# Two attention layers on one core: the parts of queries and keys go from one on-chip buffer straight into the score operands, without a copy in device memory

## Time and profile before

| | us |
|---|---|
| median of 3 runs (3643.35 to 3670.59) | 3657.52 |
| the profiled execution, its own time | 3658.99 |
| its span, first to last instruction | 3657.2 |
| PE busy, share of the span | 3449.0 (94%) |
| DVE busy | 2872.1 (79%) |
| ACT busy | 2484.4 (68%) |
| POOL busy | 2119.5 (58%) |
| bytes moved by DMA | 376.45 MB, mean 103 GB/s |

### The profile page before, as it was taken

The page is one execution under the profiler, slowest core; times in us unless marked ns, Lnnn a source line. Parts: engine busy times, 40 slices in busy tenths (PEclk is TensorE's granted clock), DMA queues, the critical chain, the costliest instruction groups (busy, mean ns, idle before and its releaser), DMA issues. The chain is left out here.

```text
span 3657.2 us, 79325 instructions
## 1 busy us (share of the span) xinstructions
PE 3449.0 (94%) x26824; PEld 1944.8 (53%) x26824; DVE 2872.1 (79%) x8451; ACT 2484.4 (68%) x5347; POOL 2119.5 (58%) x2340
## 2 busy tenths in 40 slices
PE   5999999999999999999689999999999999999997
PEld 2444444444444444444446666666666666666664
DVE  5899999999998999998267777677777777777773
ACT  2788888788788888887346666566666666666663
POOL 2377777677767777775745455455454554554542
PEclk7999999999999999999879999999999999999997
DMA  4344434433343444343466767767668668677761
GB/s 122 68 83 86 95 68 90 93 87 76 84 99 71 89 88 92 71 87 91 87 130 106 139 120 122 134 118 124 129 120 132 116 120 142 118 121 139 122 108 30
DMA packets 251934, 376.45 MB, mean 103 GB/s; under 512 B 21930, under 2 KB 122448, under 8 KB 251264
## 3 DMA queue, kind: packets, MB, share of 16 engines
q1 hardware_dynamic: 249484, 369.28, 53.2%
q10 hardware_dynamic: 2048, 2.10, 0.4%
HBM read 223.97 MB, written 136.95 MB: 99 GB/s over the span
## 5 line engine op out<-in xcount | busy, mean ns | idle before, releaser
L681 DVE TENSOR_REDUCE maxima<-ps_max 128x1 f32<-128x512 f32 x2048 | 1274.1, 680 | 98.2 <-PE ps_max L444 94.0
L1524 DVE CUSTOM_DVE_ANT_0 ps_max<-ps_max,mask 128x512 f32<-128x512 f32 (+3 forms) x2048 | 962.4, 515 | 353.4 <-PE ps_max L1246 350.7
L575 ACT ACTIVATE probs<-ps_rest 128x512 f32<-128x512 f32 x2048 | 1073.5, 602 | 226.7 <-PE ps_rest L457 224.1
L1397 ACT ACTIVATE probs<-ps_rest 128x512 f32<-128x512 f32 (+3 forms) x2048 | 773.4, 436 | 452.4 <-PE ps_rest L1267 400.0
L444 PE MATMUL ps_max<-k_op,q_op 48*128 48x512 f32 x2048 | 724.5, 446 | 61.8 <-DVE maxima L681 54.0
L457 PE MATMUL ps_rest<-q_op,k_op 50*128 50x512 f32 x2048 | 717.1, 441 | 0.3 <-ACT probs L575 0.2
L444 PEld LDWEIGHTS ps_max<-k_op,q_op 48*128 48x128 f32 x2048 | 340.2, 187 | 531.7 <-DVE maxima L681 411.5
L1246 PE MATMUL ps_max<-k_op,q_op 51*128 51x512 f32 (+3 forms) x2048 | 564.6, 366 | 23.8 <-DVE maxima L1524 4.0
L1267 PE MATMUL ps_rest<-q_op,k_op 53*128 53x512 f32 (+3 forms) x2048 | 559.6, 366 | 19.9 <-DMA q_op<-mrows 19.7
L478 PE MATMUL ps_pv<-probs,v_op 128*32 128x512 f32 x4096 | 543.0, 605 | 1.0 <-ACT oT L587 1.0
L1246 PEld LDWEIGHTS ps_max<-k_op,q_op 51*128 51x128 f32 x2048 | 315.4, 188 | 166.9 <-DVE maxima L1524 89.6
(11 more groups left out here) (145 smaller groups left out, 5465.3 us busy)
## 6 DMA issues: line engine op xcount, KB each, us to landing
qk_parts<-qparts SPq DMA_DIRECT2D x192, 512.0 KB, 3.2
q_op<-qk_parts SPq DMA_DIRECT2D x384, 256.0 KB, 7.8
k_op<-qk_parts SPq DMA_DIRECT2D x192, 256.0 KB, 10.5
xin<-in_x SPq DMA_DIRECT2D x32, 512.0 KB, 4.6
xres<-in_x SPq DMA_DIRECT2D x32, 512.0 KB, 4.8
x_mid<-xo SPq DMA_DIRECT2D x32, 512.0 KB, 3.2
xin<-x_mid SPq DMA_DIRECT2D x32, 512.0 KB, 7.1
xres<-x_mid SPq DMA_DIRECT2D x32, 512.0 KB, 15.8
```

Source lines behind the costliest of these rows:

```text
L575: act.activation(probs[:, quad % 2, at:at + S], ps_rest[:, bank("exp", b, p), :], ACT.Exp).then_inc(ps_out["exp"], 1)
L681: dve.tensor_reduce(at, ps_max[:, bank("max", c, k), :], AX.X, ALU.max).then_inc(ps_out["max"], 1)
L1397: act.activation(probs[quad % 2][:, at:at + nq], ps_rest[:, bank("exp", b, p), 0:nq], ACT.Exp).then_inc(ps_out["exp"], 1)
L1524: dve.tensor_tensor_reduce(row, row, mask[:, S - keys:S], 1.0, LOWEST, ALU.add, ALU.max, at).then_inc(ps_out["max"], 1)
```

## The change

The weights of the query and key projections are reordered on the host so that within each 128 output columns the dimension of a head is the slow index and the head the fast one (`by_dim`). Row p of a projection is then dimension p // 8 of head p % 8, and the 128 rows of a part, read in order, are already `[16, 8, 512]`. The loads read `qparts` on chip instead of `qk_dram`; `store_parts`, its steps in the two plans, `qk_dram` and `qk_stored` are gone. The loads wait for the splits themselves. `split_qk` now waits for the loads that read the buffer: in layer 0 those of the sequence before, in layer 1 for parts 0 and 1 those of unit 1 of the sequence before, for parts 2 and 3 those of unit 0 of the same sequence.

```diff
 PLAN_MQA
-PPP load_x:0:2 store_qk:0:1 qk:0:1
+PPP load_x:0:2 qk:0:1
-PPPP ft:0:-2 store_qk:1:1 otr:0:0
+PPPP ft:0:-2 otr:0:0
 PLAN_CAUSAL
-PPP split_qk:2:1 qk:2:1 cut_ont:0:-1 otr:2:-1 store_qk:2:1
+PPP split_qk:2:1 qk:2:1 cut_ont:0:-1 otr:2:-1
-V PPPPP ont:0:-1 split:2:0 qk:3:1 store_qk:3:1
+V PPPPP ont:0:-1 split:2:0 qk:3:1
-PPPP xt:0:2 out:0:-1 store_qk:0:2
+PPPP xt:0:2 out:0:-1
-PPP split:1:1 V store_qk:1:2 store:0:-1 ffn:0:-1 ffn:1:-1 split_qk:1:2
+PPP split:1:1 V store:0:-1 ffn:0:-1 ffn:1:-1 split_qk:1:2
@@ layer 0, load_queries
-            sp.wait_ge(qk_stored[unit], 16 * (c + 1))
+            sp.wait_ge(qk_split, c * NQK + unit + 1)
             if due(seen := (c - 1) * HEADS * NT):
                 sp.wait_ge(ps_full["exp"], seen)
             for g in range(len(Q_TERMS)):
                 at = HALF_ROWS * unit + g * DH
-                src = qk_dram[par, Q_TERMS[g], unit, :, :]
                 sp.dma_start(q_op[at:at + DH, par, :, :].bitcast(F32),
-                             src.rearrange("(h d) s -> d h s", d=DH)).then_inc(op_loaded[unit], 16)
+                             qparts[:, unit, Q_TERMS[g], :].bitcast(F32)).then_inc(op_loaded[unit], 16)
@@ layer 0, split_qk
-            if due(seen := 16 * c):
-                pool.wait_ge(qk_stored[k % 2], seen)
+            if due(seen := 16 * UNIT_LOADS * c):
+                pool.wait_ge(op_loaded[k], seen)
@@ both layers
-        def store_parts(c, par, k):
...
@@ layer 1, load_operands
-            for k in range(2):
-                sp.wait_ge(qk_stored[k], 16 * (2 * c + unit + 1))
+            sp.wait_ge(qk_split, c * NQK + 2 * unit + 2)
...
             for g in range(len(Q_TERMS)):
                 at = HALF_ROWS * unit + g * DH
-                src = qk_dram[par, Q_TERMS[g], 2 * unit, :, :]
                 sp.dma_start(q_op[at:at + DH, par, :, :].bitcast(F32),
-                             src.rearrange("(h d) s -> d h s", d=DH)).then_inc(op_loaded[unit], 16)
-                src = qk_dram[par, K_TERMS[g], 2 * unit + 1, :, :]
+                             qparts[:, 0, Q_TERMS[g], :].bitcast(F32)).then_inc(op_loaded[unit], 16)
                 sp.dma_start(k_op[at:at + DH, par, :, :].bitcast(F32),
-                             src.rearrange("(h d) s -> d h s", d=DH)).then_inc(op_loaded[unit], 16)
+                             qparts[:, 1, K_TERMS[g], :].bitcast(F32)).then_inc(op_loaded[unit], 16)
@@ layer 1, split_qk
-            if due(seen := 16 * (2 * c + k // 2)):
-                pool.wait_ge(qk_stored[k % 2], seen)
+            if due(seen := 16 * UNIT_LOADS * (c + k // 2)):
+                pool.wait_ge(op_loaded[1 - k // 2], seen)
             else:
-                pool.wait_ge(ahead["qk_stored"][k % 2], 16 * NB)
+                pool.wait_ge(ahead["op_loaded"][k], 16 * UNIT_LOADS * NB)
@@ kernel
+    def by_dim(wT):
+        return wT.reshape(D, -1, P // DH, DH).transpose(0, 1, 3, 2).reshape(D, -1)
+
+    for name in ("wq0T", "wqk1T"):
+        w[name] = by_dim(w[name])
```

More of the change, by code:

```diff
@@ L228, in sb @@
         return tiles.enter_context(nc.sbuf_tensor(f"{name}_{L}", shape, dt))
-    qk_dram = nc.dram_tensor(f"qk_parts_{L}", [2, 2, NQK, P, S], F32).ap()
     mparts = maxima.bitcast(BF16)
@@ L277, in layer_mqa @@
     kv_split = sem("kv_split")
-    qk_stored = [sem("qk_stored_0"), sem("qk_stored_1")]
     op_loaded = [sem("op_loaded_0"), sem("op_loaded_1")]
@@ L416, in body @@
                     load_maxima(b + d, (par + d) % 2, k)
-                elif kind == "store_qk":
-                    store_parts(b + d, (par + d) % 2, k)
                 elif kind == "load_k":
@@ L930, in layer_mqa @@
     sems |= {"ps_full": ps_full, "ps_out": ps_out, "stats_done": stats_done, "meanvar_ready": meanvar_ready,
-             "xn_ready": xn_ready, "qk_stored": qk_stored, "op_loaded": op_loaded}
+             "xn_ready": xn_ready, "op_loaded": op_loaded}
     return {"sync": sync, "tensor": tensor, "scalar": scalar, "vector": vector, "gpsimd": gpsimd,
@@ L1148, in load_residual @@
             sp.dma_start(xres[:, :, :], x_tiles[c]).then_inc(xres_loaded, 16)
[L1150 to L1159, removed]
         def load_operands(c, par, unit):
```

## The result

| | before | after |
|---|---|---|
| median, us | 3664.05 | 3930.55 |
| ratio, 95% interval | | 1.0734 (1.0685 to 1.0783) |
| span of the profiled execution | 3657.2 | 3920.9 |
| mean granted clock | 0.974 | 0.937 |
| turns of sequences 2 to 29, us | 1553.8 | 1778.3 |

The kernel is 7.3% slower: forecast 3870, measured 3930, inside the range of 3775 to 3950. The page of after first: the DMA total, the costliest of GpSimd's waits, and the load issues.

A forecast was written before the change was run, and what follows sets the result against it. TensorE was taken to set the pace in both layers, each late step costing its lateness. Start, 28 turns, change-over and layer 1's first turn summed as 3659.0 - 2.6 + 185 + 24 + 5 = 3870 us, range 3775 to 3950.

The forecast's parts named there:

- What is removed: 0 in the steady state, -2.6 at the start: 192 stores leave the DMA queue: 0 to -39 us in steady state; first score tile's operand loads -2.6 us.
- The loads take no other time: Loads into 16 partitions keep 123 GB/s from on chip, 12.8 us per unit; ends 5.6 and 19.2.
- Rival (a): On-chip loads run at 283 GB/s and land at 13.9 us, no stall in the turns; 3634 us, chance 0.08.
- (c): Reading and writing on chip disturb each other, 6.4 us more a unit; 4062 us, chance 0.09.
- The landing at 21.1 and the chain to 33.0: Layer 1 turns: unit 0's loads land 21.1 us in; GpSimd's splits, cuts and `norm1` behind end at 33.0.
- A stall of 6.0 less 0.4 won back: Each layer 1 turn: PE stands 6.0 us for GpSimd's chain and wins back 0.4 from its idle time.
- The maxima's waits are swallowed: Layer 1 turns: today's PE waits for the maxima's small DMAs vanish beside the new stall.
- The clock: 2.4 us a turn, at most 3.5: Layer 1 turns: PE's lower clock level adds 2.4 us beyond the stall, between 0 and 3.5.
- A turn of 62.1, +185 in 28: Layer 1, sequences 2 to 29: 54.1 + 6.0 + 2.4 - 0.4 = 62.1 us a turn; +185 in all, ends +81 and +303.
- The change-over +24: Between the layers: layer 0's rounding chain starts 24.0 us later behind the waiting split; +24, between +10 and +30.
- Sequence 0 +5, sequence 1 and the last two 0: Layer 1's ends: first turn +5, between 0 and 8; turn 1 lands before 15 us, last two lack `norm1`: 0.
- Rival (b): The wait is harmless in the turns, through earlier loads or PE's timely inputs; only the change-over pays; 3675 us, chance 0.08.

The follow-up runs named there:

- the run of layer 0 alone: The kernel before with only layer 0 on the on-chip path, layer 1 keeping its parts in device memory; 3663.1 us, ratio 0.9988.

## Why the prediction was right, and where its sizes were off

- **TensorE bounds, and each late step costs its lateness.** Right. Layer 1's turns carry 224.5 us of the loss.
- **What is removed: 0 in the steady state, -2.6 at the start.** Nearly right: the keys were issued 2.0 us sooner (39.57 against 41.56) and the first score tile came 2.3 us earlier (47.05 against 49.33). PE's wait before it is no shorter, 4.53 us, since PE had also finished its work ahead of it sooner (42.5 against 45.1). At layer 0's end -1.4 was left.
- **Layer 0's wait is free.** Right, by its turns; and the run of layer 0 alone shows no cost.
- **The loads take no other time.** Right: 8.0 and 10.6 us to landing, 122 GB/s against 123. Rival (a), by which on-chip loads would run at 283, is refuted, and (c), 6.4 us more a unit, as well. So the sentence of the Trainium skill that the prediction put beside rival (a) (SBUF — State Buffer, section "A bandwidth-pool intuition that's wrong") does not hold for these loads into 16 partitions: by these two rates the source in device memory was not their bottleneck.
- **The landing at 21.1 and the chain to 33.0.** Right: 21.5 and 33.3 in the turn shown. The threshold of 15.0 was then tried from both sides: releases around it (median 14.9) cost next to nothing, one at about 19 with the whole chain behind it cost 3.6 us of waits a turn.
- **A stall of 6.0 less 0.4 won back.** PE's waits for GpSimd's chain, `o_half` behind it among them, are (96.2 + 26.3 + 12.5) / 28 = 4.8 us a turn, where 5.6 were foretold. The forecast took PE's own arrival as fixed; but PE, waiting and working slower, reached the exponential tile of pair 34, ahead of `xt`, 27.0 us into the turn in the median and not at 25.8, and so stood less.
- **The maxima's waits are swallowed.** Wrong: 14 of them with 14.2 us remained, 0.5 a turn.
- **The clock: 2.4 us a turn, at most 3.5.** This is the term that was mis-sized, and it missed its own range: 263.5 - 149.2 = 114.3 us, 4.1 a turn. The row I took it from had 2.4 us beside a stall of 3.07; I carried over the amount, where the ratio would have been the thing: 2.4 / 3.07 * 6.0 = 4.7.
- **A turn of 62.1, +185 in 28.** Measured 54.1 + 4.8 + 0.5 + 4.1 = 63.5, +224.5. The differences are +1.7 for the clock, +0.5 for the maxima and -0.8 for the stall.
- **The change-over +24.** Right: +25.5. The experiment that moved one split shows the cause. PE's wait of 39.5 us there also came near the 38 foretold.
- **Sequence 0 +5, sequence 1 and the last two 0.** Measured +2.6, +6.4, +6.1 for sequence 30 and 0 for sequence 31. The zeros of sequences 1 and 30 were wrong: in sequence 1 PE waited 4.9 us for the maxima's DMAs, which I had not looked for there, and in sequence 30 it waited 2.5 us in all (1.8 in before); the rest went with a granted clock of 0.88.
- **Rival (b), a harmless wait,** did not come: the loads were issued 1.7 us into the turn as before, and PE stood. What it would have looked like shows in the run that waits for half of the loads, with a release around the threshold: 3662 us, where (b) was priced at 3675.
- **The range.** Its end of 3950 held, with 20 us to spare. The clock was outside its own bounds and the zeros of sequences 1 and 30 were wrong, all in the same direction; the stall, smaller than foretold, took back 22 us (28 * 0.8). So the mechanism and the place of the loss were foreseen, and the time fell inside the range although one term did not fall inside its own.

## What to carry to other kernels

When a buffer is read by a longer-lived reader than before, find what is queued behind the writer that must now wait, and compute the latest landing that still costs nothing; here 15.0 us, and a landing at 21.5 cost 7% of the kernel. Then look for the cheapest way under it: here a semaphore for each buffer, and issuing first the loads that free the buffer needed first, took back nine tenths. Price a TensorE stall at its length times 1.7 or more when a row of the same kernel shows that ratio, and before moving a burst of large loads look where the small, urgent DMAs stand.

## What the runs showed of the hardware that was not expected

- With a few microseconds of standing in each turn, TensorE's granted clock is lower although it is busy nine tenths of the time (1606.2 of 1778.3 us in after): with 5.3 us of waits a turn it was 0.92, with 1.1 us 0.99, with next to none 1.00. The two levels are 1.2 and 2.4 GHz, so a mean of 0.92 is an average of the lower one for about a sixth of the time and the full one for the rest, an estimate from that mean.
- Loads of 16 partitions gained when the partitions were spread at a stride of 3: 137 GB/s instead of 122 with the source on chip, 158 instead of 123 with the source in device memory, all queues together; the last load of a unit landed 2.5 and 2.9 us sooner in the median. This alone made the kernel before 1.25% faster.
- DMAs of 8 KB on ScalarE's queue did not get past a burst of six 256 KB loads on SP's queue. Issued at about the same time of the turn (34.6 to 35.1 us in the median), they kept PE waiting up to 5.7 us, until the burst had landed at 47, when it was issued from 31 us on; with a burst landed at 34 PE had 2.1 us of waits of any kind in 28 turns.
